# Layer 1's banded long filter moved beside the triangular substitution, and layer 0's choice search moved into the linear attention

## The reference

```python
scores = softmax(xf @ router_w + router_b)
G, idx = top_k(scores.T, K)          # K = 256 of 4096 tokens, for each expert
```

```python
A = tril(einsum('bhnid,bhnjd->bhnij', kb, kc), -1)
T = inv(eye(32) + A); u = T @ v; w = T @ kb     # 512 unit triangular matrices of 32 x 32
o, S = scan(step, S0, (q, k, u, w))              # branch 3
# branch 1: a causal filter of 3 taps over v; branch 2: one of 63 taps; branch 4: v itself
```

## Time and profile before

| | us |
|---|---|
| median of 3 runs | 3658.37 |
| lowest and highest run | 3649.19, 3660.01 |
| profiled execution | 3650.99 |
| span of its profile, first to last instruction | 3649.2 |
| busy in the span: PE, DVE, ACT, POOL | 2464.7, 2058.7, 1356.0, 794.2 |
| mean granted TensorE clock | 0.811 of full speed |

### The profile page before, as it was taken

How to read it: one execution, slowest core, us unless ns; L and a number is a source line. 1 busy time by engine, 2 the same in 40 slices (tenths; PEclk the granted TensorE clock), 3 DMA queues, 4 the chain that set the end, 5 groups by cost and what they waited for, 6 DMA issues and landing times. The chain is left out here.

```text
span 3649.2 us, 56982 instructions
## 1 busy us (share of the span) xinstructions
PE 2464.7 (68%) x19990; PEld 1766.3 (48%) x19990; DVE 2058.7 (56%) x4745; ACT 1356.0 (37%) x2364; POOL 794.2 (22%) x753
## 2 busy tenths in 40 slices
PE   6998941734150588804279999998615296978994
PEld 4655631523050588702245555556613275966773
DVE  5555567255829133354778888883345695452125
ACT  4444410332200023012158888883214332433432
POOL 0000001200057121073042000001354871114200
PEclk9999975766555799557579999999857698987997
DMA  5000000210020246210000000004510003731000
GB/s 174 1 1 0 0 2 15 66 28 3 0 61 31 47 139 204 83 41 5 20 32 17 1 2 1 1 1 136 158 41 26 20 0 106 223 109 41 29 0 28
DMA packets 156420, 172.92 MB, mean 47 GB/s; under 512 B 55333, under 2 KB 125739, under 8 KB 155595
## 3 DMA queue, kind: packets, MB, share of 16 engines
q1 hardware_dynamic: 135322, 127.39, 12.3%
q0 software_dynamic: 20912, 43.22, 3.9%
HBM read 124.61 MB, written 45.94 MB: 47 GB/s over the span
## 5 line engine op out<-in xcount | busy, mean ns | idle before, releaser
L2461 DVE CUSTOM_DVE_ANT_0 decayed_sd<-decayed_sc,decayed_decay 128x512 f32<-128x512 f32 x512 | 331.7, 686 | 85.6 <-PE decayed_sc L2338 85.4
L2416 ACT ACTIVATE decayed_pr<-decayed_sd,decayed_shift 128x512 f32<-128x512 f32 x512 | 339.0, 713 | 49.3 <-DVE decayed_shift L2468 49.0
L2350 PEld LDWEIGHTS decayed_tr<-all_ident,decayed_pr 128*128 128x128 f32 x2048 | 223.6, 140 | 175.2 <-ACT decayed_pr L2416 101.1
L2350 PE MATMUL decayed_tr<-all_ident,decayed_pr 128*128 128x128 f32 x2048 | 276.8, 278 | 11.1 <-ACT decayed_pt L2423 10.8
L460 PE MATMUL experts_up<-experts_xt,experts_w 128*128 128x256 f32 x1140 | 271.1, 384 | 0.0
L460 PEld LDWEIGHTS experts_up<-experts_xt,experts_w 128*128 128x128 f32 x1140 | 210.8, 194 | 24.4
L386 POOL DMA_INDIRECT rows_in<-L_T,all_slot x128 | 149.1, 1165 | 138.1 <-SPq L2265 82.2
L2475 DVE COPY decayed_pt<-decayed_tr 128x512 f32<-128x512 f32 x256 | 173.3, 685 | 2.6 <-PE decayed_tr L2350 2.6
L437 POOL DMA_DIRECT2D rows_out<-experts_y x121 | 87.4, 723 | 363.6 <-DVE experts_y L522 199.8
L694 PEld LDWEIGHTS moe_down<-moe_w,moe_h 128*128 128x128 f32 x1024 | 132.0, 192 | 56.6 <-issue 55.7
L2423 ACT ACTIVATE decayed_pt<-decayed_tr 128x512 f32<-128x512 f32 x256 | 138.2, 591 | 37.0 <-PE decayed_tr L2350 37.0
(11 more groups left out here) (508 smaller groups left out, 5493.6 us busy)
## 6 DMA issues: line engine op xcount, KB each, us to landing
experts_w<-in_L_experts SPq DMA_DIRECT2D x78, 384.0 KB, 3.4
experts_w<-in_L_experts SPq DMA_DIRECT2D x43, 579.0 KB, 4.0
experts_tok<-rows_in SPq DMA_DIRECT2D x121, 128.0 KB, 3.5
rows_out<-experts_y POOLq DMA_DIRECT2D x121, 128.0 KB, 3.5
fir_band<-bands SPq DMA_DIRECT2D x16, 768.0 KB, 7.6
rows_in<-linear_zero SPq DMA_DIRECT2D x43, 128.0 KB, 1.9
experts_w<-in_L_experts SPq DMA_DIRECT2D x8, 514.0 KB, 3.3
experts_b<-in_L_experts_b SPq DMA_DIRECT2D x43, 64.0 KB, 4.3
```

The costliest lines, as they stand in the source:

```text
L2350: last = pe.transpose(tr[u % TURNED][:, t * P:(t + 1) * P], pr[:, u % RING, t * P:(t + 1) * P], m.ident[:, :])
L2416: act.activation(pr[:, u % RING, :], sd[:, u % RING, :], ACT.Exp, bias=shift[:, u % RING:u % RING + 1]).then_inc(exp_ready, 1)
L2461: dve.tensor_tensor_reduce(out=sd[:, u % RING, :], in0=sc[h][:, :], in1=decay[:, qt, :], scale=1.0, scalar=-3.0e38, op0=ALU.mult, op1=ALU. ...
```

## The change

Three things. First, the search of `choice` becomes a class `Search` whose steps are called from `linear_attention_phase`: `begin` ahead of the first row, and two rounds for each row of the attention: one count ahead of the 13th K/V projection, decided after Q of the next row has been joined, and one count ahead of the last tile's transposes, decided after the last division. The counts use the banks `y` and `proj[0]`. The scores are stored by SP in that phase. Second, the 8 rows of the linear attention are all written out, and PE reads the input where it lies, without POOL's copy. Third, `fir_phase` goes away: its loads, products and copies run in `solveb`, now with groups of 4 channels in a ring of 7 (five of whose places lie in `vc`), and ACT makes all the copies. The transpose of v into `vc`, the 3-tap filter and its transpose follow the substitution on DVE. The layer's input X is written to memory in `conv` and read back in `stats`, its place being used between; the branches change places.

```diff
+    def propose(self, dve):
+        self.link(dve.tensor_tensor(self.tried[:, :, :], self.found[:, :].unsqueeze(1).to_broadcast([P, self.TRIED, self.E]), self.bits[:, :, :], ALU.bitwise_or))
+        for c in range(self.TRIED):
+            self.link(dve.tensor_tensor(self.marks[:, c], self.score[:, :, :], self.over(self.tried[:, c, :].bitcast(F32)), ALU.is_ge))
+        dve.tensor_reduce(self.part[:, :, :], self.marks[:, :, :, :].rearrange("p c t e -> p c e t"), AX, ALU.add).then_inc(self.part_ready, 1)
+    def count(self, pe, m, bank, n):
+        pe.wait_ge(self.part_ready, n + 1)
+        pe.matmul(bank[:, 0:self.TRIED * self.E], m.ones[:, :], self.part[:, :, :].rearrange("p c e -> p (c e)"), start=True, stop=True).then_inc(self.count_ready, 1)
...
         def rows(eng, body):
-            body(0, 0, False)
-            body(1, 1, False)
-            with eng.Fori(1, NB // 2 - 1) as i:
-                body(i * 2, 0, False)
-                body(i * 2 + 1, 1, False)
-            body(NB - 2, 0, False)
-            body(NB - 1, 1, True)
+            for b in range(NB):
+                body(b, b % 2, b == NB - 1)
...
                 for u in range(16):
+                    if u == 12:
+                        reached(pe, y_step, b * 2)
+                        search.count(pe, m, y, 2 * b)
+                    if u == 0 and b > 0:
+                        pe.wait_ge(search.count_read, 2 * b)
...
                 for t in range(TPB + 2):
+                    if t == TPB and not last_row:
+                        pe.wait_ge(halves, (b + 1) * PHI + 7)
+                        search.count(pe, m, proj[0], 2 * b + 1)
...
                     join_q(b + 1, 1 - slot)
+                search.decide(dve, y, 2 * b)
...
                     divide(u)
+                if not last_row:
+                    search.decide(dve, proj[0], 2 * b + 1)
                 dve.wait_ge(y_ps, b * TPB + TPB)
...
+            search.begin(dve, m)
             join_q(0, 0)
...
@@ short_conv_phase
+            sp.dma_start(spill, m.X[:, :, :]).then_inc(spilled, 16)
+            sp.wait_ge(spilled, 16)
...
@@ normalise_phase
-            link(dve.transpose(vc[:, :], v[:, :]))
...
@@ solve_phase, second block: SP
                 sp.dma_start(by_chunk(lanes[:, :])[:, q, :], a_dram[q, :, :].rearrange("q n j -> n q j")).then_inc(fetched, 16)
+            sp.dma_start(ws[:, :], d["L1_fir_short"]).then_inc(loaded, 16)
+            sp.dma_start(flip[:, :], bass.AP(m.bands.tensor, P * BAND, [[1, P], [1, P]])).then_inc(loaded, 16)
+            for g in range(GROUPS):
+                if g >= RING:
+                    sp.wait_ge(half_read, (g - RING) // 2 + 1)
+                sp.dma_start(band(g), bass.AP(m.bands.tensor, g * GROUP * BAND + 64, [[1, P], [BAND, GROUP], [1, WIDE]])).then_inc(band_loaded[g % RING], 16)
             sp.wait_ge(solved, N_STEPS)
             sp.dma_start(t_dram, products[:, :].rearrange("p (q j) -> p q j", j=32)).then_inc(sent, 16)
...
@@ solve_phase, second block: DVE, after the substitution
+            tie = chained(dve, short_step)
+            dve.wait_ge(half_read, 2 * BANKS)
+            tie(dve.transpose(vc[:, :], v[:, :]))
+            dve.wait_ge(loaded, 32)
+            dve.wait_ge(rows_sent, 1)
+            tie(dve.tensor_scalar(acc, v[:, :], ws[:, SHORT - 1:SHORT], None, ALU.mult))
+            for lag in (1, 2):
+                kept = time(acc)[:, :, lag:]
+                tie(dve.scalar_tensor_tensor(out=kept, in0=time(v[:, :])[:, :, 0:SEQ - lag], scalar=ws[:, SHORT - 1 - lag:SHORT - lag], in1=kept, op0=ALU.mult, op1=ALU.add))
+            tie(dve.transpose(v[:, :], acc))
...
@@ branch_stats_phase
+            sp.dma_start(m.X[:, :, :], spill).then_inc(back, 16)
+            sp.wait_ge(back, 16)
```

More of the change, by code:

```diff
@@ L927, in expert_choice_phase @@
         total = s.sb("total", [P, NT, E])
-        r = s.sb("r", [P, NT])
-        part = s.sb("part", [P, TRIED, E])
+        part = s.sb("part", [P, E])
         room = s.sb("room", [P, E])
-        found, added = (s.sb(x, [P, E], I32) for x in ("found", "added"))
-        bits, tried, keep = (s.sb(x, [P, TRIED, E], I32) for x in ("bits", "tried", "keep"))
         count = s.banks("count", 1)[0]
@@ L1002, in _ @@
         def _(dve):
[L1003 to L1034, removed]
             link = chained(dve, last_step)
@@ L1220, in _, with linear_attention_phase @@
             sp.wait_ge(loaded, 16 * len(pairs))
-def linear_attention_phase(nc, phase, m, d, out, before):
+def linear_attention_phase(nc, phase, m, d, out, before, search):
     PAIRS, DH = 8, 64
@@ L1710, in solve_phase @@
         row = s.sb("row", [P, HEADS, 31])
+        SHORT, WIDE, GROUP, RING, LENT = 3, 192, 4, 7, 5
+        GROUPS, PER_BANK = P // GROUP, 512 // NT
+        BANKS = P // PER_BANK
+        ws, flip = s.sb("ws", [P, SHORT]), s.sb("flip", [P, P])
+        lent, own = vc[:, 0:LENT * GROUP * WIDE].rearrange("p (r c w) -> p r c w", r=LENT, c=GROUP), s.sb("band", [P, RING - LENT, GROUP, WIDE])
+        band = lambda g: lent[:, g % RING] if g % RING < LENT else own[:, g % RING - LENT]
+        turned, ps = s.banks("turned", 2), s.banks("ps", 2)
+        spread = s.enter_context(nc.psum_tensor(f"{phase}_spread", [P, TPB, 512], F32))
+        band_loaded = [s.sem(f"band_loaded{r}") for r in range(RING)]
+        loaded, turned_ps, vt_kept, half_read, y_kept, spread_ps, fl_kept, rows_sent, short_step = map(
+            s.sem, ("loaded", "turned_ps", "vt_kept", "half_read", "y_kept", "spread_ps", "fl_kept", "rows_sent", "short_step"))
+        by_tile = lambda x: x.rearrange("p (c n) -> p c n", n=NT)
+        time = lambda x: x.rearrange("p (b x) -> p b x", b=BATCH)
         fetched, solved, sent, back = map(s.sem, ("fetched", "solved", "sent", "back"))
@@ L1716, in _ @@
         def _(pool):
-            if send is not None:
-                send(pool)
+            send(pool)
+            pool.sem_inc(rows_sent, 1)
+        @block.tensor
+        def _(pe):
+            for n in range(NB):
+                if n >= 2:
+                    pe.wait_ge(vt_kept, n - 1)
+                for x in range(TPB):
+                    at = (n * TPB + x) * P
+                    last = pe.transpose(turned[n % 2][:, x * P:(x + 1) * P], v[:, at:at + P], m.ident[:, :])
+                last.then_inc(turned_ps, 1)
+            pe.wait_ge(vt_kept, NB)
+            for x in range(BANKS):
+                if x >= 2:
+                    pe.wait_ge(y_kept, x - 1)
+                for half in range(2):
+                    pair = [g for g in range(4 * x + 2 * half, 4 * x + 2 * half + 2)]
+                    for g in pair:
+                        pe.wait_ge(band_loaded[g % RING], 16 * (g // RING + 1))
+                        for c in range(g * GROUP, (g + 1) * GROUP):
+                            at = c % PER_BANK * NT
+                            pe.matmul(ps[x % 2][:, at:at + NT], band(g)[:, c % GROUP, 64:WIDE], by_tile(vt)[:, c, :],
+                                      start=(c % PER_BANK == 0), stop=False, skip_group_check=True)
+                    for g in pair:
+                        for c in range(g * GROUP, (g + 1) * GROUP):
+                            at = c % PER_BANK * NT
+                            later = ps[x % 2][64:P, at:at + NT].rearrange("p (b t) -> p b t", t=TPB)[:, :, 1:]
+                            sooner = by_tile(vt)[64:P, c, :].rearrange("p (b t) -> p b t", t=TPB)[:, :, 0:TPB - 1]
+                            last = pe.matmul(later, band(g)[64:P, c % GROUP, 0:64], sooner, start=False, stop=True, skip_group_check=True)
+                    last.then_inc(half_read, 1)
+            pe.wait_ge(y_kept, BANKS)
+            pe.wait_ge(loaded, 32)
+            for half in range(2):
+                for j in range(4):
+                    if half == 1:
+                        pe.wait_ge(fl_kept, j + 1)
+                    for h in range(HEADS):
+                        c = h * HD + half * PER_BANK
+                        last = pe.matmul(spread[32 * h:32 * h + 32, j, :], flip[:, 32 * j:32 * j + 32], y[:, c * NT:c * NT + 512], start=True, stop=True)
+                    last.then_inc(spread_ps, 1)
@@ new lines, in _ @@
+        @block.scalar
+        def _(act):
+            for n in range(NB):
+                act.wait_ge(turned_ps, n + 1)
+                act.activation(by_tile(vt)[:, :, n * TPB:(n + 1) * TPB].rearrange("p c t -> p t c"),
+                               turned[n % 2][:, :].rearrange("p (t c) -> p t c", c=P), ACT.Copy).then_inc(vt_kept, 1)
+            for x in range(BANKS):
+                act.wait_ge(half_read, 2 * x + 2)
+                act.activation(y[:, x * 512:(x + 1) * 512], ps[x % 2][:, :], ACT.Copy).then_inc(y_kept, 1)
+            for half in range(2):
+                for j in range(4):
+                    act.wait_ge(spread_ps, half * 4 + j + 1)
+                    act.activation(fl.rearrange("p (n j d) -> p j d n", n=NT, j=4)[:, j, half * PER_BANK:(half + 1) * PER_BANK, :],
```

(17 more changed lines are left out.)

240 lines of the change are left out of this document (78 added, 162 removed).

## The result

| | before | after |
|---|---|---|
| median | 3659.19 us (4 runs) | 3541.02 us (4 runs, 3538.98 to 3545.06) |
| span of the profile | 3649.2 us | 3537.2 us |
| ratio | | 0.9678, 95% interval 0.9659 to 0.9696 |

Faster by 3.2%, but 73 us above the forecast and outside its range. To find the place I took, in both traces, the first or last instruction of the same tiles. What lies between two marks is a stretch of the program, and each stretch has its own term in the forecast.

What follows compares the result with a forecast made beforehand. It took phases to follow one another, each leaving engines idle: DVE-PE chain in the search, DVE in the substitution, PE in `fir`. Terms summed to -185.2 us from 3650.99, giving 3465.8, stated as 3468; range 3456 to 3492 us.

Steps and rivals of the forecast that it cites:

- its rounds hidden: Linear attention: DVE's share of two search rounds per row fits its idle gaps, 0 us, up to 64.5 if uncovered.
- counts: Linear attention: PE's counts for the search rounds, partly on the path, cost +3.4 us, between 0 and 9.3.
- start: Linear attention: `begin` on DVE ahead of the first join of Q costs +1.0 us, between 0 and 7.
- rows written out: Linear attention: four rows taken out of the loop gain 0.94 us each, -3.75 us in all.
- counts nearly free: Linear attention: rival that PE hides the counts behind other work, 3462 us; chance 0.16.
- Fetch of A: `solveb`: the first seven band groups, issued behind the fetch on its queue, delay it +1.0 us, between 0 and 8.4.
- filter and tail beneath the substitution: `solveb`: PE's and ACT's filter work hides beneath DVE's substitution, DVE's 20.1 us tail in a 22.6 us gap: 0 us.
- X's write and read: `conv` and `stats`: storing X and reading it back costs 0 us, at most 6.3 for the reading.
- The bands disturb the fetch: `solveb`: rival that band loads slow the fetch of A, or X's return the gathers, up to 3480 us; chance 0.13.
- a round doesn't fit: Linear attention: rival that second-gap rounds lie bare, 3496 us for seven, 3530 for all; chance 0.11.
- the filter doesn't fit: `solveb`: rival that filter halves take twice 5.26 us and delay the tail, +60 us, 3526 us; chance 0.06.
- all fifteen: Linear attention: worst form of the rival with bare search rounds, every round uncovered on DVE, 3530 us; rival's chance 0.11.

Runs made afterwards that it cites:

- its 32 increments: 32 semaphore increments on PE ahead of the scan's loop, against the kernel before: 3724.49 us, ratio 1.0166.
- the hidden 64 increments: 64 semaphore increments on PE behind `spread` in `solveb`, where PE waits anyway, against the kernel after: 3477.33 us, ratio to before 0.9510.
- the scan written out: PE's part of the scan as 16 written-out steps without a branch back, against the kernel after: 3554.42 us, ratio to before 0.9722.
- before with 128 increments: 128 semaphore increments on PE ahead of the scan's loop, against the kernel before: 3681.30 us, ratio 1.0056.
- after with 24 and 256: Two runs against the kernel after: 24 PE increments hidden behind the substitution, 3473.23 us; 256 ahead of the scan's loop, 3580.05 us.
- the four-step loop: PE's scan loop with four steps in an iteration and 4 iterations, against the kernel after: 3572.43 us.

## Why the prediction was wrong, step by step

- **The failed step is the one the sum left out.** It took every phase that the diff doesn't edit at its old time; `scan` went from 97.2 to 162.2 us, and the 0.02 for what I didn't think of was too little. With the loop moved by 64 instructions, nothing else changed, the time is 3477.33 us, inside the range (3456 to 3492). Moving the loop of the kernel before to the bad place costs 3724.49 - 3662.26 = 62.2 us (both medians of one series), of which some 5 are its 32 increments. Together these show the cause: the change moved code, and the loop fell where it is loaded again.
- Search removed, its rounds hidden, counts, start, rows written out: -80.1 against -78.35. The price of a count held (0.41 a row for two, forecast 3.4 / 8 = 0.43), so the rival of counts nearly free finds no support. Row 0 ends 114.76 - 113.51 = 1.25 us later, its own two counts in it, which leaves some 0.8 for the start (forecast 1.0); profiles with the same code up to there differ by 1.6. Of the 1.75 by which the sum came out better, 1.15 is luck: a shorter wait for PE further on in `choice` (2.60 us before, 1.45 after), where the prediction held all to stay as it is.
- `unit`: -4.1 against -4.45. Fetch of A, filter and tail beneath the substitution: -0.4 against +1.0. `fir` removed: -102.6 against -103.4.
- X's write and read: nothing can be seen of them, as forecast.
- None of the rivals was the one that came. "The bands disturb the fetch" and "a round doesn't fit" are refuted by the rows above; "the filter doesn't fit" too, though its time, 3526, is next to "all fifteen" rounds bare (3530) the nearest to the measured one. From the total alone either would have looked like the cause.
- With the loop resident, what remains above the forecast is mostly `causal3`: the span with the hidden 64 increments is 3475.9 us, 11.9 above 3649.2 - 185.2, and 7.5 of that is `causal3`, which takes 120.3 us in the profiled execution of before and some 128 in most others (below).

## What to carry to other kernels

When a change adds or unrolls code, look at the loops behind it: compare the packets of the instruction queue, stage by stage, with the count that loads each block once, and look at "issue" among PE's waits. A loop of many short matmuls like this one is fast only while its code is held: keep it well shorter than the 1,576 instructions that already depended on the start, or see where it starts, and move it by a few instructions placed where the engine waits anyway. And a forecast should have a term for the stages that are only moved.

## What the runs showed of the hardware

Code supply to PE: in the scan written out 48 packets of 16.4 KB came in 176.6 us, one in 3.7 us, 14 ns an instruction, with DMA nearly empty (4 to 5 GB/s in its windows). Short products from held code took 7 ns an instruction at the full clock and 9 at the half. The Trainium skill ("Runtime: NRT & Kernel Launch", section "Instruction fetch mechanics") gives PE an instruction memory of 2,048 instructions, filled in blocks of 256, and says that a taken branch to code outside of the current window of two blocks waits for its load. The packet size and the 18 to 19 us steps behind a branch agree; but a loop of 1,576 instructions ran seven iterations without a packet, which fits eight blocks and not a window of two. By the count of blocks touched above, seven stay and eight don't; what the eighth would be needed for is not shown. The same section calls the crossing of a block mostly hidden; here the measurement decides otherwise, 11.0 us a step against 7.4 from held code at the same clock.

A semaphore increment on PE took 0.154 to 0.157 us where it stood on the path.

`causal3` has two main durations, whatever the kernel: 120.1 to 120.3 us in the profiles of before, of before with 128 increments, of after with 24 and 256, and of the four-step loop, 125.5 in one, 127.7 to 128.7 in the others. POOL's copies there take 0.4 or 1.5 us, and the timeline of the kernel after shows which:

```profile
2784.24 1.67 DVE L2761 TENSOR_TENSOR causal_weighed<-causal_sums,L3a_qkv 128x1152 f32<-128x1152 f32 x1 [8.23 <-ACT causal_sums L2749]
2784.64 1.54 POOL L2721 COPY causal_kv<-L3a_qkv 128x128 f32 x1
2787.95 0.41 POOL L2721 COPY causal_kv<-L3a_qkv 128x128 f32 x1
2788.19 1.34 DVE L2761 TENSOR_TENSOR causal_weighed<-causal_sums,L3a_qkv 128x1152 f32<-128x1152 f32 x1
```

The slow copy starts while DVE's product is running, the fast one ahead of it. It is so for all 32 copies: the 16 slow ones start during such a product, and none of the 16 fast ones does. With 256 increments, where `causal3` takes 120.3 us, 10 copies meet a product. So what the two engines do at the same time goes with the duration of the stage; why they meet more often in one execution than in another was not tried. Runs of one kernel also lie some 8 us apart (before, in one series: 3650.64 to 3652.09 and 3658.17 to 3660.45), but each kernel has one profile, so that this is the reason is not shown.
